# The last Gram elements of one image pair fetched as single elements, and their solve moved into the next round

## The reference

```python
G = D.T @ D + DIAG_EPS * jnp.eye(N)
h_bar = (D.T @ X).T
h = h_bar
for k in range(1, K_MAX + 1):                      # K_MAX = 5
    scores = jnp.abs(h * (~mask))
    index = jnp.argmax(scores, axis=1)
    mask = mask.at[bidx, index].set(True)
    if k > 1:
        G_stack = G[I, index[:, None]]             # k-1 Gram elements of a patch
        ...                                        # one more row of the Cholesky factor L
    I = jnp.concatenate([I, index[:, None]], axis=1)
    h_stack = jnp.take_along_axis(h_bar, I, axis=1)
    x_stack = ...                                  # two triangular solves
    h = h_bar - jnp.einsum('bk,bkn->bn', x_stack, G[I])
coeffs = zeros.at[bidx, I].set(x_stack)
...
x = x + conv(gn(x));  x = x + patches_back(D @ coeffs)
```

## Time and profile before

| | |
|---|---|
| median of 3 runs | 557.24 us (556.25, 557.24, 561.85) |
| the profiled execution | 556.41 us, its span 554.6 us |
| DVE busy | 481.7 us, 87% of the span |
| PE busy | 412.5 us, 74% |
| ACT busy | 308.4 us, 56% |
| POOL busy | 149.9 us, 27% |
| mean granted TensorE clock | 0.905 of full speed |
| DMA | 50.72 MB, 91 GB/s on average |

### The profile page before, as it was taken

The page is one execution under the profiler, slowest core; times in us unless marked ns, Lnnn a source line. Parts: engine busy times, 40 slices in busy tenths (PEclk is TensorE's granted clock), DMA queues, the critical chain, the costliest instruction groups (busy, mean ns, idle before and its releaser), DMA issues. The chain is left out here.

```text
span 554.6 us, 7595 instructions
## 1 busy us (share of the span) xinstructions
PE 412.5 (74%) x1666; PEld 298.4 (54%) x1666; DVE 481.7 (87%) x2477; ACT 308.4 (56%) x682; POOL 149.9 (27%) x162
## 2 busy tenths in 40 slices
PE   0089886898683978989875789898849446788584
PEld 0032772465563854448764645466749335676453
DVE  4484669989999899999999899999999999999980
ACT  2544445687576284798646648686704343465123
POOL 3000025433200244534100554523004545330010
PEclk9999997989888778999987888999889978899788
DMA  5979212889400138999400465513102744134164
GB/s 99 173 110 167 58 38 74 135 134 153 75 2 0 32 76 156 168 139 164 103 1 1 110 161 122 130 48 83 33 1 57 165 115 100 59 76 93 22 128 99
DMA packets 110205, 50.72 MB, mean 91 GB/s; under 512 B 103633, under 2 KB 104145, under 8 KB 110161
## 3 DMA queue, kind: packets, MB, share of 16 engines
q1 hardware_dynamic: 102000, 26.13, 28.7%
q0 software_dynamic: 8160, 24.13, 18.8%
HBM read 34.24 MB, written 8.65 MB: 77 GB/s over the span
## 5 line engine op out<-in xcount | busy, mean ns | idle before, releaser
L357 POOL DMA_INDIRECT rows<-gram,idx_u x128 | 131.6, 1028 | 346.3 <-DVEq L962 316.7
L385 PE MATMUL h<-rows,diag 128*128 128x256 f32 x640 | 163.5, 416 | 51.1 <-ACT diag L643 51.1
L385 PEld LDWEIGHTS h<-rows,diag 128*128 128x128 f32 x640 | 131.9, 210 | 83.8 <-issue 63.5
L643 ACT ACTIVATE diag<-ident,dx 128x128 f32<-128x128 f32 x320 | 96.8, 387 | 52.4 <-DVEq L1054 45.2
L975 DVE SCALAR_TENSOR_TENSOR junk<-mask,rows 128x256 bf16<-128x256 bf16 x320 | 114.1, 422 | 0.0
L634 ACT ACTIVATE score<-h 128x512 f32<-128x512 f32 x80 | 47.2, 598 | 101.2 <-PE h L385 101.1
L385 PE MATMUL h<-d_sb,z 128*128 128x256 f32 x256 | 69.5, 438 | 5.0 <-DVEq L906 4.1
L915 DVE MAX8 top<-score 128x8 f32<-128x256 f32 x160 | 63.5, 417 | 8.1 <-ACT score L634 7.3
L385 PEld LDWEIGHTS h<-d_sb,z 128*128 128x128 f32 x256 | 64.6, 329 | 10.1 <-issue 5.2
L385 PE MATMUL back_ps<-coef_t,d_t 128*128 128x256 f32 x224 | 59.3, 424 | 11.8 <-ACT coef_t L649 11.8
L975 DVE SCALAR_TENSOR_TENSOR junk<-mask,h 128x256 bf16<-128x256 bf16 x160 | 65.3, 416 | 0.0
(11 more groups left out here) (142 smaller groups left out, 476.2 us busy)
## 6 DMA issues: line engine op xcount, KB each, us to landing
xa<-in_x SPq DMA_DIRECT2D x64, 128.0 KB, 5.3
out<-x SPq DMA_DIRECT2D x64, 128.0 KB, 2.9
x<-y POOLq DMA_DIRECT2D x14, 512.0 KB, 4.7
xb<-in_x SPq DMA_DIRECT2D x42, 128.0 KB
rows<-gram,idx_u POOLq DMA_INDIRECT x128, 3.0
xb<-in_x SPq DMA_DIRECT2D x14, 120.0 KB
rows<-in_x SPq DMA_DIRECT2D x6, 128.0 KB, 4.3
d_sb<-in_L_conv_dictionary SPq DMA_DIRECT2D x4, 128.0 KB, 3.9
```

What stands on the lines that cost most here:

```text
L357: pool.indirect_dma_start(out=rows[s][:, k, t, :], out_offset=None, in_=gram_dram[:, :], in_offset=bass.IndirectOffsetOnAxis(ap=idx_u[s][: ...
L385: return nc.tensor.matmul(dst, lhs, rhs, start=start, stop=stop, skip_group_check=skip)
L643: last = nc.scalar.activation(diag[s][:, t, j, :], ident[:, :], ACT.Copy, scale=dx[s][:, k, t, j:j + 1])
```

## The change

In rounds 0 to 2, at the last step (k = 4) of set 0, the 16 Gram picks are not made. DVE works out the addresses of the 16 elements (`g_place`, one operation) and POOL fetches them from DRAM with 16 indirect transfers of one element per partition. The picks of `h` go to a tile of their own (`h_last`). The ten operations of that solve run in the next round, in the first scan of set 1. The spreads of the round before can therefore not start at the round's end and move: image 0 to the select of set 1 at k = 0, image 1 to the select of set 0 at k = 1, image 2 behind the extract of set 0 at k = 1, image 3 to the select of set 1 at k = 1. The work that follows a spread on PE, ACT and POOL moves one place later too, image by image. The buffer `dx` gets a sixth place so that the late solve may write while the new round writes its own.

```diff
+            def gather_elements(r):
+                pool.wait_ge(g_placed, r + 1)
+                flat = gram_dram.rearrange("m (n a) -> (m n) a", a=1)
+                for t in range(TILES):
+                    for j in range(STEPS - 1):
+                        pool.indirect_dma_start(out=g_at[0][:, t, j:j + 1], out_offset=None, in_=flat,
+                                                in_offset=bass.IndirectOffsetOnAxis(ap=g_place[:, j, t:t + 1], axis=0)
+                                                ).then_inc(g_in, 16)
...
-            added_after = {(0, 1): 0, (1, 1): 1, (3, 1): 2}
+            added_after = {(1, 1): 0, (3, 1): 1}
...
+                if r < ROUNDS - 1:
+                    gather_elements(r)
+                if r > 0:
+                    add_back(IMG_R * (r - 1) + 2)
... PE
-                if behind:
-                    coef_transposes(b, 0)
                 correlate(r, 1)
                 if front:
                     x_sums(f)
-                if behind:
-                    reconstruct(b, 0)
                 update(r, 0, 0)
                 if behind:
-                    coef_transposes(b, 1)
-                    reconstruct(b, 1)
+                    coef_transposes(b, 0)
+                    reconstruct(b, 0)
                 update(r, 1, 0)
...
                 update(r, 1, 3)
                 if front:
                     correlate(f, 0)
+                if behind:
+                    coef_transposes(b, 3)
+                    reconstruct(b, 3)
... ACT
                 scores(r, 1, 4)
                 if front:
                     norm_y(f, 2)
                     norm_y(f, 3)
                     scores(f, 0, 0)
+                if behind:
+                    copy_coef(b, 3)
+                    out_back(b, 3)
... DVE, select
+                if by_element(r, s, k):
+                    now = idx_u[s][:, k, :].rearrange("p (a t) -> p a t", a=1).to_broadcast([P, k, TILES])
+                    c = step(v.scalar_tensor_tensor(out=g_place[:, :, :], in0=idx_u[s][:, 0:k, :], scalar=float(ATOMS),
+                                                    in1=now, op0=ALU.mult, op1=ALU.add))
+                    after(c)
+                    dve.sem_inc(g_placed, 1)
... DVE, extract and solve
-                for j in range(k):
+                for j in range(0 if late else k):
...
+                if late:
+                    dve.wait_ge(g_in, 16 * (STEPS - 1) * TILES * (r + 1))
... DVE, body
+                late = solve(r - 1, 0, STEPS - 1) if behind else nothing
...
-                    rows_of = spread(r - 1, 3) if behind and k == 1 else nothing
+                    rows_of = spread(r - 1, 1) if behind and k == 1 else nothing
...
+                    if k == 0:
+                        beside[2] = together(late, beside[2])
+                    if k == 1 and behind:
+                        run(spread(r - 1, 2))
                     scan(r, 1, k, together(chain[0], beside[2]), 0)
-                    if k == 0 and behind:
-                        rows_of = spread(r - 1, 2)
+                    if k < 2 and behind:
+                        rows_of = spread(r - 1, 3 * k)
...
-                run(chain[1], rows_of)
-                if front:
-                    run(spread(r, 1))
+                run(chain[1])
```

More of the change, by code:

```diff
@@ L113, in build_program @@
         c_neg = [sb(f"c_neg{s}", [P, TILES]) for s in range(2)]
-        dx = [sb(f"dx{s}", [P, STEPS, TILES, STEPS]) for s in range(2)]
+        dx = [sb(f"dx{s}", [P, STEPS + 1, TILES, STEPS]) for s in range(2)]
+        h_last = sb("h_last", [P, TILES])
+        g_place = sb("g_place", [P, STEPS - 1, TILES], U32)
         x_last = [sb(f"x_last{s}", [P, TILES, STEPS]) for s in range(2)]
@@ L221, in image_parts, with dx_of, by_element @@
                                                      xa[inner, m, 0:1], b[inner, GR - 1:GR])]
+        def dx_of(r, s, k):
+            return dx[s][:, STEPS if k == 0 and r % 2 else k]
+        def by_element(r, s, k):
+            return r < ROUNDS - 1 and s == 0 and k == STEPS - 1
         def hold(eng, signal, value):
@@ L642, in diags @@
                     for j in range(k + 1):
-                        last = nc.scalar.activation(diag[s][:, t, j, :], ident[:, :], ACT.Copy, scale=dx[s][:, k, t, j:j + 1])
+                        last = nc.scalar.activation(diag[s][:, t, j, :], ident[:, :], ACT.Copy, scale=dx_of(r, s, k)[:, t, j:j + 1])
                     last.then_inc(diag_ready[s], 1)
@@ L703, in body @@
                         x_statistics(f, m)
-                if behind:
-                    copy_coef(b, 0)
                 scores(r, 1, 0)
@@ L709, in body @@
                 diags(r, 0, 0)
-                if behind:
-                    out_back(b, 0)
                 if front:
@@ L997, in extract @@
                 for t in range(TILES):
-                    if k == 0:
+                    if k == 0 or late:
                         after(marked[t])
-                    pick(r, s, t, k, h[s][:, t, :], h_at[s][:, t:t + 1])
+                    pick(r, s, t, k, h[s][:, t, :], h_last[:, t:t + 1] if late else h_at[s][:, t:t + 1])
                     next(other, None)
-                    if k > 0:
+                    if k > 0 and not late:
                         next(chain)
@@ L1012, in solve @@
                     after(picked_h[s])
[L1013 removed]
+                    c = step(v.tensor_scalar(dx_of(r, s, 0)[:, :, 0], h_at[s][:, :], -1.0, None, ALU.mult))
                     yield
@@ L1018, in solve @@
                 w = n_inv[s][:, :, 0:k, 0]
-                after(picked_g[s])
+                late = by_element(r, s, k)
+                if late:
+                    dve.wait_ge(g_in, 16 * (STEPS - 1) * TILES * (r + 1))
+                else:
+                    after(picked_g[s])
                 g_b = g_at[s][:, :, 0:k].rearrange("p t (a j) -> p t a j", a=1).to_broadcast([P, T, k, k])
@@ L1043, in solve @@
                 after(c)
-                after(picked_h[s])
-                c = step(v.scalar_tensor_tensor(out=c_neg[s][:, :], in0=h_at[s][:, :], scalar=-1.0, in1=rd[s][:, :, k],
+                if not late:
+                    after(picked_h[s])
+                h_now = h_last if late else h_at[s]
+                c = step(v.scalar_tensor_tensor(out=c_neg[s][:, :], in0=h_now[:, :], scalar=-1.0, in1=rd[s][:, :, k],
                                                 op0=ALU.mult, op1=ALU.mult))
@@ L1055, in solve @@
                 else:
-                    step(v.tensor_reduce(x_last[s][:, :, :], dx[s][:, :, :, :].rearrange("p k t j -> p t j k"), AX.X, ALU.add))
+                    step(v.tensor_reduce(x_last[s][:, :, :], dx[s][:, r % 2:r % 2 + STEPS, :, :].rearrange("p k t j -> p t j k"),
+                                         AX.X, ALU.add))
             def spread(r, m):
```

36 lines of the change are left out of this document (20 added, 16 removed).

## The result

The changed kernel takes 624.52 us (median of 4 runs, 623.41 to 625.77) against 557.65 us before (median of 4, one more than above): a ratio of 1.117, 95% interval 1.114 to 1.121. It is slower, as forecast, but by 67 us and not by 37, and above the range of 574 to 606. The profiled execution took 623.41 us with a span of 621.6 (before: 556.41 and 554.6), so the spans differ by 67.0 us.

A forecast was written before the change was run, and what follows sets the result against it. DVE was taken as the bound, busy 87% of the span, with the removed picks mostly filling a wait. Turns -13.9, put-off work +27.3 and late load +24.3 gave +37.7 us, so 594.5 us, range 574 to 606.

The forecast's parts named there:

- What bounds the kernel; the picks don't show: DVE, busy 87%; at k = 4 a 4.7 us wait for scores replaces the picks, so the scan starts 0.8 us earlier.
- The turns give 13.9 us: Turns between rounds 0/1, 1/2 and 2/3 end 5.6, 3.4 and 4.9 us earlier, 13.9 us together.
- Element gathers: POOL's 16 one-element gathers per turn, taken at a row gather's pitch, need 20.5 us and hide, adding nothing.
- rival (c): Element gathers at 2.5 us each make the late solve wait 7 to 10 us in each turn: 623 us, chance 0.05.
- What comes back, 27.3 us: Spreads and late solve operations put off into k = 0 and 1 of the next round cost DVE 3 x 9.1 us.
- The load that is now late: Rounds 1 and 2: late add holds store, store holds `xb` load; set 1's k = 2 scan waits 12.1 us, 24.3 together.
- The sum: -13.9 + 27.3 + 24.3 = +37.7 us on the profiled 556.4 us, given as 594.5 us.

The follow-up runs named there:

- the mended kernel: Changed kernel with a landing wait after each four element gathers and SP's store between the loads of the second and third image: 567.72 us, ratio 1.018.
- the late adds alone: Kernel before with only the three add-backs on GpSimd moved one place later: 588.46 us, ratio 1.058.
- the kernel with pauses: Changed kernel with one edit, GpSimd waiting after each four element gathers until those have landed: 597.86 us, ratio 1.070.

## Why the prediction was wrong, step by step

- **What bounds the kernel; the picks don't show.** Right. The scan at k = 4 waits for its scores in the place of the picks (3.59 and 2.71 us in the turn 0/1, 4.87 in 1/2, forecast 4.7; the rows stand below), and leaving out the picks alone brings 1.7 us of 16.6. DVE's busy time falls by 9.7 us, not by some 16; without picks and nothing else moved it falls by 16.1 (481.7 to 465.6), so perhaps the moved solves and spreads overlap less with other DVE work; that is not shown. DVE's rows in the changed kernel, turns 0/1 and 1/2:

```profile
161.92 0.75 DVE L939 MAX8 top<-score 128x8 f32<-128x256 f32 x2 [3.59 <-ACT score L659]
...
165.38 0.76 DVE L939 MAX8 top<-score 128x8 f32<-128x256 f32 x2 [2.71 <-issue]
...
306.65 0.75 DVE L939 MAX8 top<-score 128x8 f32<-128x256 f32 x2 [4.87 <-issue]
```
- **The turns give 13.9 us.** Right as a term, 16.9 in the mended kernel, with -3.8, -5.3 and -7.9 for -5.6, -3.4 and -4.9. The last is the one that was sized too low. In the changed kernel itself none of it is seen, because of the next step.
- **"Element gathers", and rival (c).** The failed step. It prices the gathers by their own pitch (1.28 us forecast, 1.25 measured) and asks only whether they are through in time. They were: 16 from 156.27 to 176.19, and the late solve did not wait for them. Rival (c) has 623 us, close to what was measured, but by gathers of 2.5 us and a waiting solve, and neither is there: its number agrees by luck. What cost 26.5 us is that sixteen in a row without a stop keep back the signals of PE and DVE, a price that the sum has at nothing. No row bore on it: the kernel before never issues more than four gathers in a row, at most with an add behind each four, and the bounds were taken from the price of one. The estimate worked out from the fixed cost in the Trainium skill (DMA: Bandwidth & Descriptors, Anatomy of one DMA — SWDGE; 2.0 us each, 32 us for 16 if they did not overlap) is also not what happened: they were through in 21 us. And the add took 4.7 us in rounds 1 and 2, not the 3.2 estimated from the same rule.
- **What comes back, 27.3 us.** Right as a sum: the rounds of the mended kernel take 28.3 us more, and 22.3 of the 23.4 us of spreads come back when they are left out there. Its reason, that the spreads stood exactly where DVE would otherwise wait, holds for a third of them: in the kernel before the waits cover 8.2 of their 23.4 us, and the rest comes back as shorter turns.
- **"The load that is now late", 24.3 us.** Right in mechanism, place and order of links, too low in size: 15.9 us for each of two rounds and not 12.1, 29 to 32 us in all. Of the 3.2 us by which the third MAX8 is later than forecast, 0.9 is the gathers ahead of the add, 1.3 the load (8.3 for 7.0) and 1.2 the way from diags to scores (8.0 for 6.8), less 0.2 at the store. Both of the last two were taken from rows with other neighbours: a load that followed no store in SP's queue, and an update at a granted clock of 0.75 where it was 0.59 here. The store alone does not make the load's 8.3 us: with the late adds alone it took 7.5 (232.29 to 239.80) behind the same store.
- **The sum.** Forecast -13.9 + 27.3 + 24.3 = 37.7. Measured, by kernels against before: 9.8 for turns and put-off work together (forecast 13.4), 29.2 for the late load, 26.5 for the run of gathers, 65.5 in all. Without the last it is 39, and the kernel with pauses, 597.86 us, lies 3.4 us from the forecast.

## What to carry to other kernels

Break a series of indirect gathers issued by GpSimd into groups of four or so with something between them (a wait for landing or about 2 us of other work of GpSimd), and when a wait has no plausible releaser, look for such a series on GpSimd beside it. When a kernel makes something later, follow the in-order queues behind it link by link; here the places of three adds were worth 30 us. And before work is taken off the busiest engine, ask whether it stands in front of a wait; before it is put off, whether the place where it lands has one.

## What the runs showed of the hardware that was not expected

- Sixteen indirect gathers issued by GpSimd one each 1.25 us hold back semaphore updates of PE by up to some 10 us and DVE's, even those for itself, by up to 2.3; ACT's never by more than 0.03. Behind eight gathers PE's are up to 4.0 us late, in part of the cases, behind four at most 1.6. 4 and 512 bytes for each partition act alike (25 and 27 us over three series), and a stop of 1.5 to 2.2 us after each four takes the cost away. PE's and DVE's operations have their usual length meanwhile.
- An element gather of 4 bytes for each partition costs as much of GpSimd's time as one of 1 KB: 0.94 to 1.1 us, pitch 1.25 us.
- A load of `xb` (four transfers of 128 KB at most), from its issue to the operation that it released, took 8.3 to 8.8 us directly behind a store in the same queue in the changed kernel and its variants without gathers and with pauses, 7.4 and 7.5 us behind a store in the kernel with the late adds alone, and 6.8 to 7.5 us where no store stood directly ahead.
- The same update of 24 matmuls took 5.42 us at a granted clock of 1.00 and 8.40 us at 0.64, in two executions in which PE had stood 1.9 and 2.8 us before it.
